# Attention pass of a graph network: the index lists of gathered groups are asked for five groups further ahead than the destination rows

## The reference

```python
h = (x @ W).reshape(N, H, D)
a_src = jnp.einsum('nhd,hd->nh', h, att_src)
a_dst = jnp.einsum('nhd,hd->nh', h, att_dst)
alpha = leaky_relu(a_src[src] + a_dst[dst], 0.2)
alpha = jnp.exp(alpha - amax[dst])
alpha = alpha / (segment_sum(alpha, dst) + 1e-16)
out = segment_sum(h[src] * alpha[:, :, None], dst)
return out.reshape(N, H * D) @ Wl + bl
```

## Time and profile before

| | us |
|---|---|
| median of 3 runs | 11772.17 (11768.04 to 11773.39) |
| the profiled execution, its own time | 11778.97 |
| its span | 11777.2 |
| mean granted TensorE clock in it | 0.743 |

### The profile page before, as it was taken

One profiled execution on the slowest core, in us unless ns is written; L12 is line 12 of the kernel. 1 busy time (PEld: TensorE's weight loads), 2 busy tenths in 40 slices (PEclk: granted clock), 3 DMA queues, 4 the chain that ended last, 5 costly groups with the idle time before them and its releaser, 6 DMA issues.

```text
span 11777.2 us, 251712 instructions
## 1 busy us (share of the span) xinstructions
PE 7183.2 (61%) x60627; PEld 5309.9 (45%) x60628; DVE 5143.7 (44%) x13946; ACT 1762.1 (15%) x3566; POOL 5592.2 (47%) x5555
## 2 busy tenths in 40 slices
PE   5666666666366666677864444555666455555666
PEld 4555555555222111345543334444566454444566
DVE  4444455454787777444332223333322333322333
ACT  2333333232123455100000000000000000000000
POOL 3666655554100000565027777776543665643654
PEclk9777777777698999788985555566777676666777
DMA  2222222222111223455542222224556566555566
GB/s 59 67 64 64 63 60 65 59 59 55 31 55 76 108 127 136 165 154 159 181 131 51 54 53 57 58 60 127 174 186 210 176 245 237 172 203 192 194 225 200
DMA packets 977745, 1416.35 MB, mean 120 GB/s; under 512 B 540705, under 2 KB 649761, under 8 KB 970914
## 3 DMA queue, kind: packets, MB, share of 16 engines
q1 hardware_dynamic: 689858, 1130.79, 28.1%
q0 software_dynamic: 184832, 224.29, 8.7%
q10 hardware_dynamic: 102752, 58.62, 1.7%
HBM read 1197.73 MB, written 215.36 MB: 120 GB/s over the span
## 4 chain that ended last, share of the span: by engine, by line
PE 29%; issue 22%; DVE 16%; DVEq 14%; POOL 11%; DMA 7%; ACT 1%; SPq 1%; POOLq 0%; ACTq 0%
PE ps_turn L925 13%; POOL ARENA L622 11%; PE ps_out L778 4%; PE ps_turn L882 4%; DMA ARENA<-table_gat,idx 3%; DMA ARENA<-counts 2%; DVE onehots L1720 2%; DVEq L1734 2%; DVE ARENA L1637 2%; PE ps_pair L778 1%; DVE ARENA L1635 1%; DMA idx<-src_r 1%; PE ps_pair L953 1%; PE ps_turn L694 1%; DVEq L394 1%
## 5 line engine op out<-in xcount | busy, mean ns | idle before, releaser
L622 POOL DMA_INDIRECT ARENA<-table_sage,idx x1920 | 1894.5, 987 | 1735.6 <-DVE idx L1715 1198.0
L925 PE MATMUL ps_turn<-ARENA 128*128 128x96 bf16 (+2 forms) x24010 | 2273.2, 262 | 541.8 <-DVE DSUM L1766 202.1
L925 PEld LDWEIGHTS ps_turn<-ARENA 128*128 128x128 bf16 x24010 | 1861.7, 106 | 948.6 <-issue 648.5
L622 POOL DMA_INDIRECT ARENA<-table_gat,idx x1568 | 1660.0, 1059 | 1203.2 <-issue 1150.7
L622 POOL DMA_INDIRECT ARENA<-table_gine,idx x1568 | 1539.0, 982 | 965.1 <-issue 954.1
L882 PE MATMUL ps_turn<-ARENA 128*128 128x392 bf16 (+1 forms) x4204 | 1060.8, 357 | 674.7 <-DVE ARENA L1637 478.4
L622 POOL DMA_INDIRECT ARENA<-table_dev,idx x480 | 479.8, 1000 | 1754.0 <-DVE idx L1715 1617.5
L953 PE MATMUL ps_pair<-ARENA,onehots 128*128 128x32 bf16 (+2 forms) x10140 | 700.5, 227 | 995.4 <-DVE ARENA L1727 833.1
L778 PE MATMUL ps_out<-ARENA,onehots 128*128 128x256 f32 (+1 forms) x3136 | 939.8, 468 | 508.6 <-DMA ARENA<-table_gine,idx 364.4
L1635 DVE TENSOR_SCALAR ARENA<-ARENA 128x784 bf16<-128x784 f16 (+1 forms) x2102 | 1008.2, 480 | 360.0 <-issue 234.0
L778 PE MATMUL ps_pair<-ARENA,onehots 128*128 128x256 f32 (+1 forms) x3136 | 888.7, 448 | 386.6 <-DMA ARENA<-table_gine,idx 297.4
(11 more groups left out here) (300 smaller groups left out, 6584.9 us busy)
## 6 DMA issues: line engine op xcount, KB each, us to landing
ARENA<-counts SPq DMA_DIRECT2D x1470, 448.0 KB
counts<-ARENA SPq DMA_DIRECT2D x49, 3136.0 KB, 9.0
ARENA<-counts SPq DMA_DIRECT2D x490, 224.0 KB
ARENA<-dst_b SPq DMA_DIRECT2D x393, 256.0 KB
ARENA<-edge_attr SPq DMA_DIRECT2D x390, 128.0 KB
ARENA<-table_sage,idx POOLq DMA_INDIRECT x1920
ARENA<-table_gat,idx POOLq DMA_INDIRECT x1568
ARENA<-table_gine,idx POOLq DMA_INDIRECT x1568
```

Source lines behind the costliest of these rows:

```text
L622: pool.indirect_dma_start(ps["buf"][:, s, c, 0:ps["row"]], None, ps["table"][:, :], bass.IndirectOffsetOnAxis(idx[:, s, c:c + 1], 0)).then ...
L925: last = pe.matmul(ps_dense[half][:, 0:n], RING[:, b, :], XP[:, b, :], start=(b == PIECE_AT[pieces[0]]), stop=(j == pieces[-1] and b == PI ...
```

## The change

SyncE's loop of the attention pass is split: the request for an index list gets a function of its own, five lists are asked for before the loop, and within the loop list g + 5 is asked for ahead of destinations g + 1. The last round stands written out, since for its last five groups no list is left. `AHEAD` is 5. The conditions of both waits, the slots, the semaphores and the loops of all other engines stay. The pass with edge features uses the new function in the same order as before.

```diff
+AHEAD = 5
...
+                def load_idx(s, g):
+
+                    sp.wait_ge(ps["slots_free"], g + (order * GROUPS + 1))
+                    sp.dma_start(idx[:, s % SLOTS, :], src_r[:, bass.ds(g * C, C)]).then_inc(idx_loaded[s % SLOTS], 16)
+
                 def one(i, s, edges):
                     g = i * SLOTS + s
-                    sp.wait_ge(ps["slots_free"], g + (order * GROUPS + 1))
-                    sp.dma_start(idx[:, s, :], src_r[:, bass.ds(g * C, C)]).then_inc(idx_loaded[s], 16)
-                    if ps["name"] == "gat":
-                        load_dst(s + 1, g + 1)
+                    load_idx(s, g)
...
                 if ps["name"] == "gat":
                     load_dst(0, 0)
-                if ps["name"] != "gine":
-                    with sp.Fori(0, ROUNDS) as i:
+                    for s in range(AHEAD):
+                        load_idx(s, s)
+                    with sp.Fori(0, ROUNDS - 1) as i:
                         for s in range(SLOTS):
-                            one(i, s, P)
+                            load_idx(s + AHEAD, i * SLOTS + (s + AHEAD))
+                            load_dst(s + 1, i * SLOTS + (s + 1))
+                    for s in range(SLOTS):
+                        if s + AHEAD < SLOTS:
+                            load_idx(s + AHEAD, (ROUNDS - 1) * SLOTS + s + AHEAD)
+                        load_dst(s + 1, (ROUNDS - 1) * SLOTS + s + 1)
                 else:
```

## The result

The changed kernel takes 11544.38 us (median of 4 runs, 11537.38 to 11566.34) against 11770.10 us (11764.57 to 11773.39): a ratio of 0.9815, 95% interval 0.9801 to 0.9829, so 226 us less. Measured twice more, in e8 and e12, it was 11557.64 us (0.9829, 0.9811 to 0.9847) and 11559.87 us (0.9821, 0.9807 to 0.9834), 202 and 210 us less than the kernel before beside it. The forecast was 11,548 us, 224 us less. One number of the prediction's text is a slip: the profiled execution of before, less 224 us, is 11,555 us and not 11,755; the forecast didn't use it. One reading is off too: VectorE's last instruction of group 42 ended at 424.49, not 424.06, and the wait of 4.36 us begins there; no term changes by it.

What follows compares the result with a forecast made beforehand. The prediction took late gathers, an 11.3 us chain against two groups of lead, as the bound: 0.62 x 361.5 = 224 us off, other terms 0, giving 11,548 us from the 11772.17 median; range 11,400 to 11,670.

Steps and rivals of the forecast that it cites:

- What bounds the kernel: Attention pass: no single engine but handovers; a chain of 11.3 us from list request to rows makes VectorE wait 361.5 us.
- How much comes back: VectorE's wait for gathered rows in the attention pass: 224 us of 361.5 come back, ends 145 and 361.5 us.
- The share of a wait that returns: From two waits followed, 0.85 and 0.4, weighted by TensorE's clock to 0.62 of VectorE's wait for rows.
- the accumulation's wait for TensorE: Sign: VectorE's wait for TensorE at L1454 (L1463 after) grows from 162 us to over 200.
- The unnamed waits at the start of a group: VectorE's waits at L1505 that the profile doesn't name, register refill and loop's way back: stay at 331.6 us.
- GpSimd's own pace: GpSimd's gathering in plain rounds of the attention pass: costs 0, at most 88 us, made up at node blocks.
- The line that was to show the forecast wrong: VectorE still waiting 100 us or more for gathers at L1505 (L1514 after); under 60 us was expected.
- The other sign: GpSimd's wait for index lists in the attention pass, 43.8 us before, would be gone.
- Longer gathers: A denser VectorE could lengthen GpSimd's gathers through the shared port pair; every gather at 1.61 us would need 2,995 us.
- The destinations: SyncE's destination requests, now behind a list, leave up to 0.6 us later: costs 0, at most 235 us.
- TensorE's clock: Fewer gaps may keep TensorE at 2.4 GHz more often; left out of the sum, granted clock expected within 0.05 of 0.74.
- its rival with 425 us: All 361.5 us come back plus 65 us at L1454 from a quicker TensorE: about 425 us off, 11,347; chance 0.14.

Runs made afterwards that it cites:

- e8: The changed kernel with no edit, measured again: 11557.64 us, ratio 0.9829 to the kernel before.
- e12: The changed kernel with no edit, measured once more: 11559.87 us, ratio 0.9821 to the kernel before.
- e1: The changed kernel with a lead of one list in place of five, lists asked for about three groups ahead: 11557.50 us, ratio 0.9827.
- e5: The kernel before, with two of four gathers of a group left out from the second round on in the attention pass: 11513.75 us, ratio 0.9786.
- e6: The changed kernel with a quarter of the attention pass's 256-wide matmuls left out: 11473.16 us, ratio 0.9755.
- e3: The changed kernel with two of four gathers of a group left out from the second round on in the attention pass: 11475.04 us, ratio 0.9751.
- e4: The changed kernel with VectorE's wide multiplication (128 x 1024) cut into four of 128 x 256: 11530.53 us, ratio 0.9808.
- e7: The changed kernel with VectorE's wide multiplication cut into two of 128 x 512: 11553.82 us, ratio 0.9823.
- e2: The changed kernel with a lead of six lists in place of five, so destinations leave later: 12050.26 us, ratio 1.0244.
- e11: The changed kernel with the wide multiplication in four pieces in the first 13 rounds, whole after, VectorE's round standing twice behind a branch: 11650.32 us, ratio 0.9895.
- e9: The changed kernel with four multiplication pieces in the first 13 rounds, whole after, behind a branch, on a slower chip: 15130.64 us, ratio 1.0007.
- e10: The changed kernel with destinations g + 1 requested before list g + 5 in all rounds but the last, on a slower chip: 15120.83 us, ratio 1.0004.

## Why the prediction was right, point by point

*What bounds the kernel.* Right, and shown: the chain of 11.3 us against a lead of two groups. One more group of lead (e1) or a shorter chain (e5) removes most of the wait.

*How much comes back.* The sum was right, 224 us forecast and 226 measured (202 and 210 in e8 and e12), but that it came out so close is luck: two of its terms were off and made up for each other. The share of a wait that returns was put at 0.62, from two groups followed. In the 287 groups where GpSimd keeps ahead it was 167 / 220.5 = 0.76. What replaced the rest was not the accumulation's wait for TensorE: expected above 200 us, it stayed at 165. The unnamed waits at the start of a group, which were to stay at 331.6 us, took its place. Of their growth of 60 us, 22 lie at the fifth group of a round, where the registers are refilled, and 36 in the groups without a refill, where they went from 19 waits to 81, in three lengths of 0.2, 0.6 and 1.3 us. Some of 0.2 and 1.3 us stood in before too, so it is likely that they had run under the wait for rows; what they are isn't shown. TensorE's wait at L820 fell from 255.8 to 230.1 only, not "well below". e6 shows TensorE as part of the bound, at 0.45 us for each us of its work. SyncE's wait didn't stay at L476 either: most of it went to the lists.

*GpSimd's own pace.* This step of the sum failed. It was put at 0, 88 us at most, because "it makes it up at each node block, of which there is one every 3.5 rounds". That is the mean. The first block comes after 14 rounds, and in the first 13 there is no store to draw on. There GpSimd paces VectorE: 587.0 / 104 = 5.6 us a group, and four gathers of 1,092 ns with their pauses are 4 x (1.09 + 0.30) = 5.6 us. e3 prices it at 70 us. The line that was to show the forecast wrong, 100 us or more of waiting at L1514, was nearly reached (90.0), and the wait that was expected, under 60 us, was passed. The other sign, that GpSimd's wait for lists would be gone, came true in the first 104 groups alone (0.3 us). By the share of the later groups the first part should have given 0.76 x 140.9 = 107 us, and it gave 43: 64 us stayed with GpSimd, close to what e3 gives by another way. A share of 0.76 in place of 0.62 is worth 51 us more, GpSimd's pace 64 us less: so 224 became 211 us in this pass.

*Longer gathers.* The slow ones went from 237 to 311 of 1,564, and e4 and e7 show that they follow the length of VectorE's instruction. This agrees with the rule of the Trainium skill that was weighed (SBUF — State Buffer, section SBUF: two separate sides): GpSimd is held while VectorE has the shared port pair. The other direction isn't seen: the multiplication kept to 1,218 ns on average, 1,265 at most. That a denser VectorE makes more gathers long, as the prediction said it could, came true, and it is a part of GpSimd's pace.

*The destinations.* 0 was right: 0.7 us of waiting for them. e2 shows how near the edge is.

*TensorE's clock.* The granted clock in the pass went from 0.74 to 0.76 (0.77 in e8 and e12), and its rival with 425 us didn't happen. The rule of the Trainium skill that was named (TensorE: Matmul & The Clock Gate, section HAM oscillation — how this bites in real kernels) has the right sign: with fewer waits for DMA the granted clock is higher, by 0.02 to 0.03. Why by so little isn't shown; VectorE's stalls at the first group of a round stayed as they were (284 and 286 us). e6 shows the other side: with a quarter of the matmuls gone the clock fell to 0.70, and the ones left got longer.

## What to carry to other kernels

Compare the length of a prefetch chain, from the request to the last landing, with the shortest run of steps inside its lead, not with the mean: one step of lead too few cost 361 us of waiting here, and one more was enough. A request's real condition can be hidden behind another that stands ahead of it in the same queue; move it as far forward as its own condition comes first, and not one further. Where a store is to carry a slower engine, look for the longest stretch without a refill.

## What the runs showed of the hardware that was not expected

- A gather that usually takes 0.94 us takes up to 2.13 us beside VectorE's 128 x 1024 multiplication of 1.22 us, and up to 2.65 us beside its 128 x 1792 one of 2.02 us (L1260), once a node block; with the former in four pieces of 418 ns, 104 of 1,564 are over 1.2 us, with one of 1,218 ns 311.
- The multiplication takes 1,218 ns in one piece, 2 x 684 in two (e7) and 4 x 418 in four (e4): 0.15 us for each further piece.
- A branch over a second copy of VectorE's round goes with 2.8 us more idle time a round (e11), about half of the 6.0 us that VectorE stands idle at the first group of a round, where its loop goes back.
- On the chip of e9 and e10 the kernel before took 15,105 us. VectorE was busy there for about the same time (5,131 us in e10, 5,149 in the changed kernel), with longer waits between the engines. The two kernels that hold the change were not faster there. Why is open.
